# Causal attention inside a two-layer transformer kernel: the exponentials' blocks ordered by halves of the queries, and four output projections moved into the last step

## What is computed

```python
x = x + attn_a(layernorm(x))      # 16 heads of 16, one shared key/value head, causal
x = x + ffn(layernorm(x))         # shared expert of 1024 + 8 routed experts, top 2
x = x + attn_b(layernorm(x))      # 16 heads of 16 with ALiBi bias, causal
x = x + ffn(layernorm(x))
# in both attentions, for each head:
scores = q @ k.T / sqrt(16); scores[j > i] = -inf
out = softmax(scores) @ v
result = concat(out) @ w_fc (+ b_fc)
```

## Time and profile before

| | us |
|---|---|
| three executions | 1126.43, 1129.21, 1132.49 |
| median | 1129.21 |
| the profiled execution | 1143.65 |
| its span | 1141.8 |
| TensorE busy in the span | 1035.0 (91%) |
| steady step (fifth step of the first layer) | 29.74 |
| fifth step of the second layer (its diagonal masks are made by TensorE) | 31.97 |

### The profile page before, as it was taken

The page is one execution under the profiler, slowest core; times in us unless marked ns, Lnnn a source line. Parts: engine busy times, 40 slices in busy tenths (PEclk is TensorE's granted clock), DMA queues, the critical chain, the costliest instruction groups (busy, mean ns, idle before and its releaser), DMA issues. The chain is left out here.

```text
span 1141.8 us, 20106 instructions
## 1 busy us (share of the span) xinstructions
PE 1035.0 (91%) x6848; PEld 656.1 (57%) x6848; DVE 790.4 (69%) x1584; ACT 591.4 (52%) x1258; POOL 404.2 (35%) x426
## 2 busy tenths in 40 slices
PE   4799999999998898999887999999999887989998
PEld 3433333333376788888775343434334776888877
DVE  7898788887366754448687978887873757544465
ACT  6317677777743335533253367776676333355332
POOL 3503632323535215345553002321235442163361
PEclk9859999999998999999899799999999988999999
DMA  4550111110033224533149423332211421245351
GB/s 132 148 84 17 36 40 35 36 40 27 25 106 139 66 84 145 132 109 94 46 137 184 81 46 61 69 62 57 57 27 27 144 96 57 74 144 140 111 159 54
DMA packets 65380, 94.99 MB, mean 83 GB/s; under 512 B 20575, under 2 KB 49183, under 8 KB 62929
## 3 DMA queue, kind: packets, MB, share of 16 engines
q1 hardware_dynamic: 44549, 52.28, 17.7%
q10 hardware_dynamic: 13820, 22.54, 7.3%
q0 software_dynamic: 6912, 18.88, 6.3%
HBM read 66.33 MB, written 26.67 MB: 81 GB/s over the span
## 5 line engine op out<-in xcount | busy, mean ns | idle before, releaser
L1200 ACT ACTIVATE pt<-st_ps 128x512 f32<-128x512 f32 (+3 forms) x768 | 327.4, 493 | 187.8 <-PE st_ps L846 112.2
L846 PE MATMUL st_ps<-qs,ks 99*128 99x512 bf16 (+7 forms) x768 | 243.0, 330 | 8.0 <-ACT pt L1200 5.6
L1439 DVE TENSOR_REDUCE mab<-su_ps 128x1 f32<-128x512 f32 (+2 forms) x288 | 181.5, 662 | 28.1 <-PE su_ps L826 19.9
L603 POOL TENSOR_SCALAR_AFFINE_SELECT pt<-pt 128x512 f32<-128x512 f32 x112 | 71.1, 635 | 341.5 <-ACT pt L1200 341.5
L864 PE MATMUL o_ps<-pt,vp 128*32 128x512 f32 (+3 forms) x1536 | 163.6, 498 | 1.9 <-POOL pt L603 1.0
L822 PE MATMUL su_ps<-ks,qs 96*128 96x512 bf16 (+5 forms) x448 | 159.0, 370 | 2.9 <-DVE mab L1439 1.6
L846 PEld LDWEIGHTS st_ps<-qs,ks 99*128 99x128 bf16 (+1 forms) x768 | 73.3, 98 | 113.2 <-ACT pt L1200 63.3
L680 POOL DMA_INDIRECT rows_in<-rows,source x80 | 76.3, 954 | 154.0 <-PE st_ps L1037 70.2
L1226 ACT CAST hh<-hf 128x512 fp32r<-128x512 f32 x64 | 39.7, 620 | 168.7 <-DVE hf L1640 160.9
L178 PE MATMUL st_ps<-xt_h,wu 128*128 128x512 f32 x256 | 103.5, 404 | 6.3 <-DVE xt_l L1364 3.7
L179 PE MATMUL st_ps<-xt_h,wu 128*128 128x512 f32 x256 | 102.4, 400 | 0.0
(11 more groups left out here) (220 smaller groups left out, 2132.7 us busy)
## 6 DMA issues: line engine op xcount, KB each, us to landing
wu_raw<-w_units_dram SPq DMA_DIRECT2D x32, 384.0 KB
outs<-rows_out ACTq DMA_DIRECT2D x40, 256.0 KB
qs<-q_parts ACTq DMA_DIRECT2D x60, 128.0 KB
q_parts<-hml SPq DMA_DIRECT2D x16, 384.0 KB, 3.3
wexp_raw<-w_units_dram SPq DMA_DIRECT2D x16, 384.0 KB, 6.6
qs<-q_parts SPq DMA_DIRECT2D x36, 128.0 KB
inv<-inverses SPq DMA_DIRECT2D x128, 32.0 KB, 1.8
rows<-xn SPq DMA_DIRECT2D x8, 512.0 KB, 6.3
```

Of the source, the lines that this page charges most:

```text
L603: pool.affine_select(block, block, [[0, 4], [1, P]], ALU.is_ge, 0.0, base=0, channel_multiplier=-1).then_inc(masked, 1)
L846: last = pe.matmul(bank[KM_BANKS[n % len(KM_BANKS)]][:, lo - CH * part:hi - CH * part], key_stack(l, s)(j)[0:rows, P * kt:P * kt + P], qs[ ...
L1200: act.activation(pt[:, kt % 2, j, lo:hi], bank[KM_BANKS[i % len(KM_BANKS)]][:, lo - CH * part:hi - CH * part], ACT.Exp, scale=1 / np.sqrt( ...
L1439: dve.tensor_reduce(to, bank[SU_BANKS[n % len(SU_BANKS)]][:, 0:share * width].rearrange("p (j k) -> p j k", j=share), AX.X, ALU.max).then_ ...
```

## The change

The list of blocks goes by halves of the queries: (0,0) (1,0) (2,0) (3,0), then (0,1) to (7,1). LAST_QUAD, last_quad, the spreading of the units and the waits are all computed from that list. Both divisions of the step before now stand behind the mask of key tile 3. In the last step the eight projections of batch 0 begin at piece 2 instead of 10, and the projections of tiles 8 to 11 (the first half of the queries of batch 1) stand behind pieces 40, 42, 44 and 46, instead of behind the transpositions in between. GpSimd's extra work of the last step stands all behind the mask of key tile 3; the square roots of chunk 2 are taken before the split of unit 2; VectorE's order in between is changed to suit.

```diff
--- before.py
+++ after.py
@@ -87,7 +87,7 @@
 NSU = len(SU) + 1
 
 
-QUADS = [(kt, part) for kt in range(QT) for part in range(kt // HALF, 2)]
+QUADS = [(kt, 0) for kt in range(HALF)] + [(kt, 1) for kt in range(QT)]
 PIECES = 4 * len(QUADS)
 LAST_QUAD = (QUADS.index((HALF - 1, 0)), QUADS.index((QT - 1, 1)))
 
@@ -126,10 +126,10 @@
 
 UNITS_BEFORE, *UNITS_BEHIND = units_behind_pieces(0.2)
 
-FC_BEHIND = {10 + 3 * t: t for t in range(QT)}
+FC_BEHIND = {**{2 + 3 * t: t for t in range(QT)}, **{40 + 2 * t: QT + t for t in range(HALF)}}
 PV_LAG = 2
 PV_BEHIND = 1
-INVERT_AT, DIVIDE_BEHIND = (6, 27), (2, 4)
+INVERT_AT, DIVIDE_BEHIND = (6, 27), 3
 
 QKV = [[("kv", 0), ("q", 0), ("q", 1)],
        [("q", 0), ("q", 1), ("k", 0), ("k", 1), ("v", 0), ("v", 1)]]
@@ -605,22 +605,18 @@
                             add_bias(2 * kt, 2 * kt + 2)
                         if s == STEPS - 1:
                             last_step(l, kt)
-                        elif s and kt in DIVIDE_BEHIND:
-                            divide(l, s - 1, DIVIDE_BEHIND.index(kt))
+                        elif s and kt == DIVIDE_BEHIND:
+                            divide(l, s - 1, 0)
+                            divide(l, s - 1, 1)
 
             def last_step(l, kt):
 
-                if kt == 0:
+                if kt == 3:
                     split_unit(l, 0)
-                if kt == 1:
                     divide(l, STEPS - 2, 0)
-                if kt == 2:
                     split_unit(l, 1)
-                if kt == 3:
                     divide(l, STEPS - 2, 1)
-                    rstds(2 * l + 1, 0, 1)
-                if kt == 4:
-                    rstds(2 * l + 1, 1, 2)
+                    rstds(2 * l + 1, 0, 2)
 
             def divide(l, s, part):
                 b, g = divmod(s, G)
@@ -693,8 +689,9 @@
                         rstds(2, 0, 2)
 
             def feed_forward(f):
+                rstds(2 * f + 1, 2, 3)
                 split_unit(f, 2)
-                rstds(2 * f + 1, 2, 4)
+                rstds(2 * f + 1, 3, 4)
                 split_unit(f, 3)
                 for e in range(POOL_EXPERTS):
                     split_expert(f, e)
@@ -934,8 +931,6 @@
                 p = 2 * l + 1
                 transpose_chunk(p, 0)
                 transpose_chunk(p, 1)
-                for tt in range(QT, QT + HALF):
-                    output_projection(l, tt)
                 route(l, 0)
                 route(l, 1)
                 up(l, 0)
@@ -1506,19 +1501,19 @@
                 add_projection(l, 2)
                 add_projection(l, 3)
                 stats(p, 1)
+                invert(step_no(l, STEPS - 1), 0)
                 normalise(p, 0)
-                invert(step_no(l, STEPS - 1), 0)
                 normalise(p, 1)
                 divide_last(l, 0)
+                add_projection(l, 4)
+                add_projection(l, 5)
+                stats(p, 2)
                 lows(p, 0)
                 invert(step_no(l, STEPS - 1), 1)
                 lows(p, 1)
-                add_projection(l, 4)
-                add_projection(l, 5)
-                stats(p, 2)
+                normalise(p, 2)
                 divide_last(l, 1)
                 hidden(l, 0)
-                normalise(p, 2)
                 hidden(l, 1)
                 add_projection(l, 6)
                 add_projection(l, 7)
```

## The result

The change makes the kernel slower. The median of four executions is 1161.27 us, against 1130.84 us for the kernel before, run on the same chip: a ratio of 1.0274, with a 95% interval from 1.0241 to 1.0307. That is 30.4 us more, where 24 were forecast. The profiled execution took 1161.26 us, with a span of 1159.4.

What follows compares the result with a forecast made beforehand. TensorE, busy 29.43 of 29.74 us a step, was taken as the bound, with ScalarE's chain of 3.13 us overtaking its 2.86. 16.8 + 2.0 + 1.8 + 3.6 = 24.2 us more gave 1153 us; forecast 1145 to 1162, 8-in-10 range 1137 to 1163.

Steps and rivals of the forecast that it cites:

- The steady step: Attention step with units: claimed to grow from 29.74 to about 31.1 us, 1.39 us a step, bounds 0.7 and 2.0.
- The chain of a block that looks back two: Attention, start of one block's values to the next's when pt's place was used two blocks before: 3.13 us for 512 columns.
- the walk of the step: One steady step priced piece by piece, each product at the later of TensorE free or bank free: 31.13 us.
- The five stalls: TensorE stalls in a steady step: 0.26 at (2,0), 0.47 (3,0), 0.31 (2,1), 0.08 (3,1), 0.79 us (4,1).
- less 0.35: About 0.35 us a steady step that TensorE no longer loses before the transposition of the maxima, VectorE being done.
- The sum over the steps: Fourteen attention steps: 16.8 us for twelve, 2.0 for steps 0 and 4 of the second layer, 1.8 for loads.
- the loads: DMA issues in ScalarE's queue, in (2,0) and (3,0), second layer: about 0.4 us in four or five steps, 1.8 together.
- The last step: Last attention step with four moved projections, up to the transpositions: 35.0 us instead of 30.8, +4.2 a layer.
- The rival of the late inverses: Last step: projections or VectorE's queue wait for the inverses, holding up TensorE; margin about 2 us; 1159 us, chance 0.07.
- Behind the attention: After the attention: four projections gone, route and everything up to chunk 3's transpositions 2.4 us earlier, not 3.4.
- The waits are filled: Rival: units slide into the gaps, steps stay, end costs 0 to +2 us a layer; 1129 to 1133 us, chance 0.07.
- Faster: Rival: steps within 0.3 us, moved projections free, chunk 3 no longer waits; 1118 to 1123 us, chance 0.09.

Runs made afterwards that it cites:

- ring_new_order: The changed kernel with pt's four places taken in turn (block q uses place q mod 4), so every block looks back four: 1116.48 us, ratio 0.9894.
- values_one_earlier: The changed kernel with the values of block b issued behind the first key product of b+2, not the second: 1133.81 us, ratio 1.0033.
- before_again: The kernel before, unchanged, profiled a second time: 1133.07 us.
- end_alone: The changed kernel with the old order of blocks, so everything but the order is new: 1161.66 us against 1142.98 on that chip, ratio 1.0155.
- order_alone: The kernel before with only the new order of blocks; projections, divisions and VectorE's order as before: 1159.74 us, ratio 1.0291.
- loads_in_wide: The changed kernel with ScalarE's loads moved to pieces 1, 5, 17, 21, 25, 29, out of narrow blocks (2,0) and (3,0): 1157.21 us, ratio 1.0256.
- places_3: The changed kernel with three pt places taken in turn, so every block looks back three: 1118.18 us in one execution.
- ring_new_order_old_end: The kernel before with the new order of blocks and four pt places taken in turn, projections and end as before: 1115.95 us, ratio 0.9889.
- ring_old_order: The kernel before, old order and old end, with four pt places taken in turn, so every block looks back four: 1118.85 us, ratio 0.9919.

## Why the prediction was right, and which terms were off

**The steady step: right.** The chain of a block that looks back two was said to take 3.13 us for 512 columns and 2.33 for 256, and the walk of the step gave 31.13. Measured: 3.14 to 3.15, 2.34 and 31.49. The five stalls stand where they were put, and with the sizes given: against ring_new_order, which has the same order and units, the five intervals are 0.21, 0.47, 0.29, 0.07 and 0.79 us longer, where 0.26, 0.47, 0.31, 0.08 and 0.79 stood. (These five less 0.35 add up to 1.56, not to the 1.39 of the walk; the forecast goes by the walk.) The stall that the walk did not have is 0.30 us at the two units behind one piece; the other 0.06 is spread over the step. The walk had no term for VectorE: it let a unit start as soon as its piece was issued. That VectorE would no longer end an idle time before the transposition of the maxima was right in after, and values_one_earlier shows the stall coming back when the chain gets shorter.

**The sum over the steps: too small.** Seven steps of each layer became 12.2 and 14.8 us longer against before_again. The forecast had 9.8 and 10.8 (twelve steps of 1.4, two of 1.0, and 1.8 for the loads), 20.6 against 27.0. Of the 6.4 that are missing, 14 x 0.30 = 4.2 are the two units. The rest is in single steps: the loads, 0.6 us a step and 1.3 in the sixth step of the second layer, where 0.4 in four or five had been taken, and 0.6 in the second step of the first layer. There GpSimd splits weights ahead of the step's first mask, and the values of (0,0) start at 115.79, just behind the mask's end:

```profile
111.68 3.43 POOL L647 TENSOR_TENSOR wp_l<-wraw,wp_h 128x1536 fp32r<-128x1536 f32 x1
115.06 0.63 POOL L603 TENSOR_SCALAR_AFFINE_SELECT pt<-pt 128x512 f32<-128x512 f32 x1
```

That split delayed the same values in before as well, but since the first three blocks of the list are narrower now, they are wanted 4.8 us into a step and no longer 5.3. The prediction had counted masks as hidden from the distances of a steady step, and had not looked at what stands before the first mask of this one.

**The last step: right.** Predicted was +4.2 a layer; up to the last exponential it is +4.45 against before_again, up to the transpositions 35.34 against 30.90, +4.44. The 3.14, 3.14 and 3.09 us of the three wide blocks were measured as such. The first moved projection starts at 327.29, and the division that it needs ends at 324.10: a margin of 3.2 us, where about 2 were expected. The rival of the late inverses did not come about, and end_alone shows what it would look like: a wait of 7.64 us on TensorE, and behind it slower work at a lower granted clock.

**Behind the attention: the mechanism right, the size known only as an average.** Predicted was a gain of 2.4 us a layer from the moved projections; against before_again the time behind the last exponential fell by 1.25 and 6.5. Route starts 2.74 us behind the transpositions and not 5.1, a gain of 2.3, and chunk 3 gets it too: its transpositions start 23.3 and 25.3 us behind the last exponential in after, 25.8 and 28.5 in order_alone, 26.4 and 28.8 in before_again. Timeline, the first layer's chunk 3, in after (last exponential ends at 333.94) and in order_alone (331.18):

```profile
357.18 1.09 PE L740 MATMUL st_ps<-cst,xn 128*128 128x128 f32 x8 [0.96 <-DVE xn L1351]
```

```profile
356.98 1.09 PE L743 MATMUL st_ps<-cst,xn 128*128 128x128 f32 x8 [1.08 <-DVE xn L1356]
```

Further on, single profiles differ by more than the effect. From the last exponential of the first attention to the first of the second, after and loads_in_wide run the same code:

```profile
333.94:651.21 317.27, 282.71 (x1722) 235.20 (x1715) 213.02 (x453) 125.78 (x249) 134.27 (x119) 0.95 0.45 118
```

```profile
334.05:648.46 314.41, 279.37 (x1722) 233.35 (x1715) 212.34 (x453) 125.59 (x249) 133.82 (x119) 0.97 0.45 120
```

So the 1.25 and 6.5, each from a single pair of profiles, have an error of that size. Over the five profiles with the new order and the new end (after, loads_in_wide, values_one_earlier, places_3, ring_new_order) this stretch is 315.6 us on average, and the one behind the second attention 247.9. With the new order and the old end (order_alone, ring_new_order_old_end) they are 317.6 and 250.9. The moved projections thus give some 2.0 and 3.0 us there, near the 2.4 forecast, and take 2.9 in each last step, which is why they show in no total. With the old order and the old end (before_again, ring_old_order) the stretches are 319.1 and 252.8, so the order by itself may shorten them by 1.5 and 1.9; with two profiles against two this is not shown. The sum of all terms is 12.2 + 14.8 + 2 x 4.45 - 1.25 - 6.5 = 28.15, against a difference of the spans of 28.1.

**What was luck.** The steps were 6.4 us more than forecast, and the two stretches behind the attention were shorter by 7.75 (1.25 + 6.5), 3 us more than the 4.8 forecast. Without this second error the time would have been about 1164 us and outside the 1145 to 1162 forecast; at 1161.27 it stands just inside.

**The base.** The forecast took differences on a profile that had a 7 us longer combination of rows. Since none of the terms came from there, nothing was lost; a forecast that had priced the feed-forward part from it would have been wrong by those 7 us.

**The rivals.** "The waits are filled" is out: the values start at the chain's pace whatever stands between, and TensorE's busy time grew without new work. As "Trainium Kernel Development and Optimization" of the Trainium skill ("Reading a trace") has it, busy time of matmuls is a bad metric for how close a kernel is to its roofline. The trace agrees: 1.09 of the 1.75 us count as busy. Of the 1.1 us of stalls that the prediction saw inside the 29.43 busy ones, ring_new_order shows 0.69: it does the same 226 matmuls with TensorE busy 28.74 us. "Faster" is out for the same reason, and order_alone shows that its other half, the moved projections, brings nothing in total. By the figure of the Trainium skill for ScalarE ("ScalarE: Activation LUTs", "What ACT_TABLE_LOAD costs") the chain would be 3.20 us, an estimate. The trace does not agree: it is 3.14 where nothing else is in the way.

**What the prediction did not see** is that the loss is no property of the order. It said that the distance is the cause, and stopped there; the next thought, that the place may follow from the number of the block, makes both kernels faster: 1118.85 with the old order, 1115.95 with the new one, with no more memory. Between these two the steady step is 0.33 us shorter in the new order, but the ratios, 0.9919 and 0.9889, have intervals that overlap.

## What to carry to other kernels

When the order of blocks changes, write down for each block how many blocks back its buffer was last used, and compare that with the lag at which the reader is issued: a reader issued two blocks behind wants a distance of three (here three gave the same step as four, and two cost 2.7 us of 28.8). Give out buffers by the running number of the block, not by a property of its index, so that the distance survives a change of order. The pace of a pipelined engine is read from the starts of one recurring instruction over a step; walked with measured prices, such a list predicted eleven of twelve intervals within 0.04 us, and the one it missed was a second engine's pace that the walk had left out.

## What the runs showed of the hardware that was not expected

- In end_alone TensorE stood still for 7.6 us; the granted clock in that stretch is 0.59, it is 0.63 in the 5.4 us of work that follow, and 1.00 (2.4 GHz) after that. A projection took 2.08 us in the slow stretch, which is close to the 1.2 GHz level, and 1.08 in after. With the slower work behind it, the wait of 7.6 us came with a last step that was 11.4 us longer, four projections included.
- A DMA issue in ScalarE's queue (0.31 and 0.44 us) holds back the exponentials behind it: 0.70 us between two starts instead of 0.27.
- The kernel before ran at 1129.4 and 1129.9 us on two chips and at 1142.98 on a third, 1.2% apart, more than some of the effects measured here. So each ratio here is to the kernel before on the same chip, and runs of different chips are compared by their ratios. Steady steps compare across chips: 29.75 us in end_alone on the third chip, 29.74 on the others.
